# Expert tiles of a mixture layer: weights as the loaded operand of gate and up, in a network kernel on one Trainium2 core

## What is computed

```
scores = einsum('bsd,ed->bse', x, w_gate_router)
topk_scores, topk_idx = top_k(scores, 2)
topk_probs = softmax(topk_scores)
weights = sum(topk_probs[..., None] * one_hot(topk_idx, E), axis=-2)
gate = einsum('bsd,efd->bsef', x, w_gate_proj)
up = einsum('bsd,efd->bsef', x, w_up_proj)
hidden = silu(gate) * up
out = einsum('bsef,edf,bse->bsd', hidden, w_down_proj, weights)
```

## Time and profile before

| | |
|---|---|
| median of 3 runs | 1829.79 us (1825.73 to 1830.11) |
| the profiled execution | 1830.81 us, span 1828.9 us |
| TensorE matmuls busy | 1611.4 us, 88% of the span |
| TensorE loads busy | 1223.2 us, 67% |
| VectorE / ScalarE / GpSimd busy | 1174.7 / 916.3 / 599.9 us |
| mean granted clock of TensorE | 0.891 of full speed |
| tile loop, gate and up of the first tile to the last eviction | 913.3 to 1079.6 us |

### The profile page before, as it was taken

The page is one execution under the profiler, slowest core; times in us unless marked ns, Lnnn a source line. Parts: engine busy times, 40 slices in busy tenths (PEclk is TensorE's granted clock), DMA queues, the critical chain, the costliest instruction groups (busy, mean ns, idle before and its releaser), DMA issues. The chain is left out here.

```text
span 1828.9 us, 77444 instructions
## 1 busy us (share of the span) xinstructions
PE 1611.4 (88%) x32043; PEld 1223.2 (67%) x32043; DVE 1174.7 (64%) x4229; ACT 916.3 (50%) x3325; POOL 599.9 (33%) x1805
## 2 busy tenths in 40 slices
PE   6999999999999999896299965788888888699999
PEld 5988999889999998896266532354545555444444
DVE  5777877777787788777644436566565666474231
ACT  5545555445455555545245445367666667532130
POOL 0333333323333333334345444133223223580000
PEclk9999999999999999555599985789888989699999
DMA  6010010200000001202446444000000000040001
GB/s 239 5 49 30 5 52 5 98 33 5 5 4 5 5 22 56 76 22 73 134 138 238 133 169 137 1 2 0 0 0 0 0 0 1 12 128 18 29 1 47
DMA packets 30635, 90.36 MB, mean 49 GB/s; under 512 B 4848, under 2 KB 6000, under 8 KB 30192
## 3 DMA queue, kind: packets, MB, share of 16 engines
q1 hardware_dynamic: 23920, 64.88, 10.4%
q0 software_dynamic: 6400, 20.98, 3.4%
HBM read 66.90 MB, written 18.87 MB: 47 GB/s over the span
## 5 line engine op out<-in xcount | busy, mean ns | idle before, releaser
L363 PE MATMUL bank<-arena 128*128 128x8 f16 x12288 | 500.9, 170 | 25.2 <-issue 14.0
L366 PE MATMUL bank<-arena 128*128 128x16 f16 x12288 | 495.2, 182 | 2.7 <-issue 2.1
L363 PEld LDWEIGHTS bank<-arena 128*128 128x128 f16 x12288 | 414.4, 97 | 57.9 <-ACT bank L459 32.0
L366 PEld LDWEIGHTS bank<-arena 128*128 128x128 f16 x12288 | 411.9, 97 | 4.1 <-issue 3.2
L635 POOL TENSOR_TENSOR arena<-arena 128x16 f32<-128x16 f32 x512 | 116.8, 228 | 565.9 <-DVE arena L566 551.2
L429 ACT ACTIVATE arena<-arena 128x16 f32<-128x16 f32 x512 | 114.4, 223 | 327.4 <-DVE arena L545 327.3
L545 DVE TENSOR_REDUCE arena<-bank 128x16 f32<-128x48 f32 x512 | 99.5, 194 | 105.2 <-PE bank L366 102.4
L556 DVE TENSOR_TENSOR_SCAN arena<-arena,bank 128x64 f32<-128x64 f32 x512 | 146.7, 287 | 21.0 <-ACT arena L429 6.9
L1898 PE MATMUL bank<-arena 128*128 128x512 f16 x704 | 152.3, 379 | 1.7 <-PEq L1419 1.7
L336 PE MATMUL bank<-arena 128*128 128x256 f16 x1008 | 150.4, 277 | 0.8 <-issue 0.7
L1454 PE MATMUL bank<-arena 128*128 128x512 f16 x576 | 144.4, 406 | 4.5 <-DVE arena L1698 4.5
(11 more groups left out here) (201 smaller groups left out, 2699.9 us busy)
## 6 DMA issues: line engine op xcount, KB each, us to landing
arena<-yrows SPq DMA_DIRECT2D x16, 512.0 KB, 4.1
arena<-in_wgu SPq DMA_DIRECT2D x8, 768.0 KB, 4.7
hrows<-arena SPq DMA_DIRECT2D x16, 256.0 KB, 4.1
arena<-in_xtok SPq DMA_DIRECT2D x16, 256.0 KB, 8.0
out_y<-arena SPq DMA_DIRECT2D x16, 256.0 KB, 2.0
arena<-in_wih SPq DMA_DIRECT2D x4, 768.0 KB, 7.5
arena<-in_whh SPq DMA_DIRECT2D x4, 768.0 KB, 5.3
arena<-in_xT SPq DMA_DIRECT2D x3, 1024.0 KB, 5.9
```

The costliest lines, as they stand in the source:

```text
L363: mm = nc.tensor.matmul(dst[:, j * B:(j + 1) * B, 1], w, h[:, 0], start=home not in opened, stop=False, skip_group_check=True)
L366: mm = nc.tensor.matmul(dst[:, j * B:(j + 1) * B, 1:3], w, h.rearrange("p a c -> p c a"), start=home not in opened, stop=False, skip_group ...
```

## The change

Three things change in the expert tiles, and the number of tiles goes from 40 to 39, the most that 4096 pairs and 8 experts can fill.

1. Gate and up take the weights as the loaded operand and x as the moving one, so that the result has the inner columns on partitions and tokens along the columns. The 384 inner columns of an expert are laid out as three blocks of 128: the first 128 of gate, the first 128 of up, and the remaining 64 of both. Each block needs 12 matmuls of 128 columns. The part pairs go in the order (0,0), (1,0), (0,1) inside each k.
2. The hidden values are then already as down needs them: `turn_hidden`, the copy to `hidT` and their semaphores go. The remaining 64 inner columns are kept as high part on partitions 0 to 63 and as low part on partitions 64 to 127 of one block, and the down weights of these columns are loaded twice, on both halves. Down is five matmuls of 128 partitions: high x high, high x low, low x high of the first 128 columns, and two of the rest block, with the high and the low weights. The elementwise work is done in a block of 128x128 and a block of 64x128 (the sigmoid and the gate product in one operation of 256 columns).
3. TensorE turns x of tile i+2 in iteration i, before down of tile i-1; VectorE copies x of tile i+2 in iteration i; ScalarE evicts tile i-1 in iteration i.

```diff
-TILES = 2 * NTOK // P + E
+FR = F - P
+TILES = (2 * NTOK + E * (P - 1)) // P
...
             if n < NDN:
-                return FH, wdn[:, 2 * n * D:2 * (n + 1) * D]
+                return P, wdn[:, 2 * n * D:2 * (n + 1) * D]
...
-                    for h_, w_ in ((0, 0), (0, 1), (1, 0)):
+                    for cols in range(3):
+                        n = 0
                         for k in range(KT):
-                            mm = nc.tensor.matmul(bank[2 + i % 2][:, 0:2 * F], xt[:, i % 2, h_ * KT + k, :],
-                                                  wgus[w_][:, k, bass.ds(e, 1), :], start=(n == 0), stop=(n == 3 * KT - 1))
-                            n += 1
+                            for h_, w_ in ((0, 0), (1, 0), (0, 1)):
+                                mm = nc.tensor.matmul(bank[2 + i % 2][:, cols * P:(cols + 1) * P],
+                                                      wgus[w_][:, k, bass.ds(e, 1), cols * P:(cols + 1) * P],
+                                                      xt[:, i % 2, h_ * KT + k, :], start=(cols == 0 and n == 0),
+                                                      stop=(n == 3 * KT - 1), skip_group_check=True)
+                                n += 1
...
-                    for h_, w_ in ((0, 0), (0, 1), (1, 0)):
-                        for half in range(2):
-                            mm = nc.tensor.matmul(bank[6 + i % 2][:, :], hidT[0:FH, i % 2, h_, half, :],
-                                                  wdns[0:FH, w_, half, bass.ds(e, 1), :], start=(n == 0), stop=(n == 5))
-                            n += 1
+                    for slot, w_, rest in ((0, 0, 0), (0, 1, 0), (1, 0, 0), (2, 0, 1), (2, 1, 1)):
+                        mm = nc.tensor.matmul(bank[6 + i % 2][:, :], hid[:, i % 2, slot, :],
+                                              wdns[:, w_, rest, bass.ds(e, 1), :], start=(n == 0), stop=(n == 4))
+                        n += 1
...
-                for i in range(TILES + 2):
+                for i in range(TILES + 1):
                     if i < TILES:
                         expert[i] = nc.tensor.value_load(own[0:1, i:i + 1], min_val=0, max_val=E - 1)
                         gate_up(i, expert[i])
                     if i == 0:
                         rest_of_tiles()
-                    if 0 < i < TILES + 1:
-                        turn_hidden(i - 1)
-                    if 0 < i < TILES - 1:
-                        turn_x(i + 1)
-                    if i > 1:
-                        down(i - 2, expert[i - 2])
+                    if i < TILES - 2:
+                        turn_x(i + 2)
+                    if i > 0:
+                        down(i - 1, expert[i - 1])
...
-                    A.activation(sg[:, i % 2, :], bank[2 + i % 2][:, 0:F], ACT.Sigmoid, scale=1 / SWX).then_inc(sig_done, 1)
+                    A.activation(sg[:, i % 2], bank[2 + i % 2][:, 0:4 * P].rearrange("p (c t) -> p c t", t=P)[:, 0:3:2, :],
+                                 ACT.Sigmoid, scale=1 / SWX).then_inc(sig_done, 1)
...
-                    A.activation(hid[:, i % 2, 0, :], hf[:, i % 2, :], ACT.Copy).then_inc(hid_hi, 1)
+                    A.activation(hid[0:FR, i % 2, 2, :], hf[0:FR, i % 2, 1, :], ACT.Copy)
+                    A.activation(hid[:, i % 2, 0, :], hf[:, i % 2, 0, :], ACT.Copy).then_inc(hid_hi, 1)
...
+                    V.scalar_tensor_tensor(hf[0:FR, i % 2, 1, :], bank[2 + i % 2][P - FR:P, 2 * P:3 * P], 1 / SW,
+                                           ga[0:FR, 1, :], ALU.mult, ALU.mult)
+                    V.scalar_tensor_tensor(hf[:, i % 2, 0, :], bank[2 + i % 2][:, P:2 * P], 1 / SW, ga[:, 0, :], ALU.mult,
                                            ALU.mult).then_inc(hf_done, 1)
...
-                    V.tensor_tensor(hid[:, i % 2, 1, :], hf[:, i % 2, :], hid[:, i % 2, 0, :],
+                    V.tensor_tensor(hid[P - FR:P, i % 2, 2, :], hf[0:FR, i % 2, 1, :], hid[0:FR, i % 2, 2, :], ALU.subtract)
+                    V.tensor_tensor(hid[:, i % 2, 1, :], hf[:, i % 2, 0, :], hid[:, i % 2, 0, :],
                                     ALU.subtract).then_inc(hid_lo, 1)
...
-                    if 0 < i < TILES - 1:
-                        take_x(i + 1)
+                    if i < TILES - 2:
+                        take_x(i + 2)
```

More of the change, by code:

```diff
@@ L29 @@
 F = 192
-FH = F // 2
-TILES = 2 * NTOK // P + E
+FR = F - P
+TILES = (2 * NTOK + E * (P - 1)) // P
 NG = NTOK // P
@@ L650, in mixed_net_kernel @@
         m = Mem(arena, mc.at)
-        wdns = m.take([2, 2, E, D], F16, FH)
+        wdns = m.take([2, 2, E, D], F16)
         rowu = m.take([TILES], F32).bitcast(U32)
@@ L703, in mixed_net_kernel @@
         xt = m.take([2, 2 * KT, P], F16)
[L704 to L708, removed]
+        hid = m.take([2, 3, P], F16)
+        hf = m.take([2, 2, P], F32)
         yo = m.take([3, D], F32)
+        ga = m.take([2, P], F32)
+        sg = m.take([2, 2, P], F32)
         assert m.at <= base + 8 * KT * GM * P
@@ L739, in mixed_net_kernel @@
         tx_mm, xt_done, gu_mm, sig_done, ga_done = sem("tx_mm"), sem("xt_done"), sem("gu_mm"), sem("sig_done"), sem("ga_done")
-        hf_done, hid_hi, hid_lo, th_mm, hT_done = sem("hf_done"), sem("hid_hi"), sem("hid_lo"), sem("th_mm"), sem("hT_done")
+        hf_done, hid_hi, hid_lo = sem("hf_done"), sem("hid_hi"), sem("hid_lo")
         yt_mm, y_evac = sem("yt_mm"), sem("y_evac")
@@ L872, in gate_up, with down @@
                         pe.wait_ge(hf_done, i - 1)
-                    n = 0
-                    for h_, w_ in ((0, 0), (0, 1), (1, 0)):
+                    for cols in range(3):
+                        n = 0
                         for k in range(KT):
-                            mm = nc.tensor.matmul(bank[2 + i % 2][:, 0:2 * F], xt[:, i % 2, h_ * KT + k, :],
-                                                  wgus[w_][:, k, bass.ds(e, 1), :], start=(n == 0), stop=(n == 3 * KT - 1))
-                            n += 1
+                            for h_, w_ in ((0, 0), (1, 0), (0, 1)):
[4 more added lines that the diff above has]
+                                n += 1
                     mm.then_inc(gu_mm, 1)
-                def turn_hidden(i):
+                def down(i, e):
                     pe.wait_ge(hid_lo, i + 1)
-                    if i >= 2:
-                        pe.wait_ge(hT_done, i - 1)
-                    for part in range(2):
-                        for half in range(2):
[L887 to L893, removed]
                     if i >= 2:
@@ L971, in high_hidden @@
                     if i >= 2:
-                        act.wait_ge(th_mm, i - 1)
-                    A.activation(hid[:, i % 2, 0, :], hf[:, i % 2, :], ACT.Copy).then_inc(hid_hi, 1)
-                def take_hidden(i):
-                    act.wait_ge(th_mm, i + 1)
-                    if i >= 2:
                         act.wait_ge(yt_mm, i - 1)
-                    A.activation(hidT[0:FH, i % 2].rearrange("p a h t -> p (a h t)"),
-                                 bank[4 + i % 2].bitcast(F16)[0:FH, 0:4 * P], ACT.Copy).then_inc(hT_done, 1)
+                    A.activation(hid[0:FR, i % 2, 2, :], hf[0:FR, i % 2, 1, :], ACT.Copy)
+                    A.activation(hid[:, i % 2, 0, :], hf[:, i % 2, 0, :], ACT.Copy).then_inc(hid_hi, 1)
                 def take_y(i):
@@ L1018, in _ @@
                 A.activation(pr[:, :, :], dif[:, :, :], ACT.Sigmoid, scale=1 / SWX).then_inc(probs, 1)
-                for i in range(TILES + 2):
+                for i in range(TILES + 1):
                     if i < TILES:
                         sigmoid(i)
-                    if 0 < i < TILES + 1:
-                        take_hidden(i - 1)
-                    if i < TILES:
                         high_hidden(i)
-                    if i > 1:
-                        take_y(i - 2)
+                    if i > 0:
+                        take_y(i - 1)
                     if i in SPLIT_IN:
@@ L1173, in hidden @@
                     dve.wait_ge(sig_done, i + 1)
-                    V.scalar_tensor_tensor(ga[:, :], bank[2 + i % 2][:, 0:F], 1 / SWX, sg[:, i % 2, :], ALU.mult,
+                    both_gates = bank[2 + i % 2][:, 0:4 * P].rearrange("p (c t) -> p c t", t=P)[:, 0:3:2, :]
+                    V.scalar_tensor_tensor(ga[:, :, :], both_gates, 1 / SWX, sg[:, i % 2], ALU.mult,
                                            ALU.mult).then_inc(ga_done, 1)
                     dve.wait_ge(ga_done, i + 1)
-                    V.scalar_tensor_tensor(hf[:, i % 2, :], bank[2 + i % 2][:, F:2 * F], 1 / SW, ga[:, :], ALU.mult,
+                    V.scalar_tensor_tensor(hf[0:FR, i % 2, 1, :], bank[2 + i % 2][P - FR:P, 2 * P:3 * P], 1 / SW,
+                                           ga[0:FR, 1, :], ALU.mult, ALU.mult)
+                    V.scalar_tensor_tensor(hf[:, i % 2, 0, :], bank[2 + i % 2][:, P:2 * P], 1 / SW, ga[:, 0, :], ALU.mult,
                                            ALU.mult).then_inc(hf_done, 1)
@@ L2011 @@
```

(6 more changed lines are left out.)

## The result

| | before | after |
|---|---|---|
| median | 1829.95 us (4 runs, 1825.73 to 1830.16) | 1855.48 us (4 runs, 1850.24 to 1858.61) |
| profiled execution, span | 1830.81, 1828.9 us | 1854.02, 1852.2 us |

The changed kernel takes 1.0142 times as long (95% interval 1.0114 to 1.0171), 25.5 us by the medians; the forecast was +22.7 us, 1852.5.

What follows compares the result with a forecast made beforehand. TensorE bounds the kernel now; after the change its sequencer would, at 4.7 us a tile against 4.03. Loop +21.5 and routing +1.2 make +22.7 us, from 1829.79 to 1852.5; own range 1843 to 1861, whole range 1838 to 1869.

Steps and rivals of the forecast that it cites:

- The number of operations: Gate and up: TensorE's sequencer makes 24 register operations a tile instead of 8, 936 over 39 tiles.
- The slot: TensorE's sequencer: each register operation takes 114 to 126 ns, taken as 125, so 16 more add 2.00 us a tile.
- TensorE's own 3.50 us: Expert tile: TensorE's stream without the sequencer, 1.98 gate and up + 0.44 x transposes + five down products of 0.216.
- The loop: Tile loop: 37 periods of 4.7 us against 4.03 now, ending at 1101.1 instead of 1079.55, +21.5 us.
- The end of the loop: Last tile: the chain after gate and up, from leaving TensorE through sigmoid and down to eviction, takes 5.3 us.
- The elementwise work: Expert tiles: VectorE 2.3 us and ScalarE 1.7 us a tile, neither near the period; it matters only in the last tile.
- The routing: Before the loop: larger down-weight loads delay ScalarE's waits for row saves by 0 to 2.0 us, taken as 1.2.
- "Issue" ahead of gate and up: Profile sign: TensorE's loads idle before gate and up by "issue", marking a late sequencer; no size given.
- Rival A: Gate and up: register operations don't grow or cost next to nothing; period 3.50 us, total 1807; chance 0.10.
- Rival C: Tile loop: TensorE's granted clock falls in the starved stream; chance 0.03.
- Rival B: Gate and up: a load-matmul pair with real weights costs more than 55 ns; at 97 ns, 1864 us; chance 0.04.

Runs made afterwards that it cites:

- e1: Changed kernel with gate and up reading weights at an address fixed in the program, so without their register operations; 1816.82 us, 0.9920 of the kernel before.
- e3: Kernel before with only 39 tiles and x turned and copied two tiles ahead; 1821.18 us, 0.9953 of the kernel before.
- e5: Kernel before with 39 tiles, x two tiles ahead and moving gate-up weights in three blocks of 128 columns (24 register operations); 1862.11 us, ratio 1.0157.
- e6: Kernel before with 39 tiles, x two ahead, three hidden-value transposes, five down products, scatter two tiles later in GpSimd's queue; 1814.02 us, ratio 0.9898.

## Why the prediction was right

- **The number of operations.** 936 at the gate-up line, 24 for each of 39 tiles, as counted from 4 k, 2 parts and 3 blocks:

```profile
L877 PEldq FUSED_REGOPS  x936: 46/46/60, 914.4 to 1098.5; - x188
```

- **The slot.** In the tile above 24 operations start within 3.0 us. The forecast of 2.8 + 2.0 - 0.13 = 4.7 met 4.70 in that tile and 4.75 in the mean from tile 1 on. The remainder is operations that start 0.15 us and more after the last instead of 0.125; I had put them in the range, not in the sum. The 24 additional pairs show no price of their own in the slots: an operation with two pairs behind it and one with a single pair both take 0.124 us in the median.
- **TensorE's own 3.50 us.** e1's tile shows 2.01 + 0.45, and the changed kernel 1.10 for down: 3.56. The trace of e1 has 56 ns per pair, over 36 pairs in a row, where the forecast took 55. In the changed kernel the spacing is 87 ns in the mean, but by e1 it is the sequencer's doing.
- **The loop.** +21.5 forecast, +22.9 measured. 37 periods at 4.75 for 4.7 make 1.9 us; the first tile and the end, together 0.5 shorter than forecast, take part of it back.
- **The end of the loop.** The last tile's chain was put at 5.3 us. The last gate-up matmul starts at 1098.6 and the last eviction ends at 1102.92 + 0.69 = 1103.6, so it took 5.0. The order of the steps is that of the prediction:

```profile
1098.84 0.38 ACT L957 ACTIVATE arena<-bank 128x256 f32<-128x256 f32 x1 [2.14 <-PE bank L877]
1099.26 0.42 DVE L1157 SCALAR_TENSOR_TENSOR arena<-bank,arena 128x256 f32<-128x256 f32 x1 [2.50 <-ACT arena L957]
...
1101.63 1.25 PE L893 MATMUL bank<-arena 128*128 x5 [1.56 <-DVE arena L1168]
1102.92 0.69 ACT L973 ACTIVATE arena<-bank,arena 128x512 f32<-128x512 f32 x1 [1.49 <-PE bank L893]
```

- **The elementwise work.** 256 columns take 425 ns on VectorE (0.42 forecast), a half of 128 takes 292 (0.29).
- **The routing was mis-sized:** +1.2 forecast, -0.6 measured. ScalarE's wait for the row saves went from 12.1 to 12.4 us only:

```profile
  DMA hrows<-arena: 12.4, 5
```

The first gather starts 58.8 us after the routing does, where it was 58.7; the 0.6 us lie behind it, as its rows were there for the first transposes after 4.2 us instead of 4.8. In the seven experiments this distance is 4.1 to 4.8 too, and e3 and e5, without the larger pieces, start the first gather after 59.3 and 57.7 us. So what the larger pieces cost is below what differs between executions, and the price of 1.2 us has nothing to show for it. I had multiplied a landing time by a number of waits without asking what each wait ended on.
- **"Issue" ahead of gate and up**, which I had named as a mark of the mechanism, is no mark: the kernel before has it too.
- **Rival A** (no growth) is what e1 shows: tiles of 3.54 us, and 1816.82 us, 10 above the 1807 of the rival, for the most part since some of its tiles wait for hidden values, which I had ruled out only for a period of 4.7. **Rival C** (the clock) didn't happen: the granted clock in the starved loop is 1.00. What a fall would have cost there, against which I had set the upper end of the whole range, no run shows. **Rival B** fell with e1, at 56 ns a pair.

## What to carry to other kernels

Count what the sequencer must do beside the matmuls. In these runs an address from a register costs TensorE's sequencer a slot of about 0.125 us for each different offset, and a wait of its own about 0.10; one or two matmuls of 128 columns at 55 ns can't cover a slot, one of 384 columns at 163 ns can. A cut into shorter matmuls with more addresses can thus lose more than the transposes and products that it saves. When TensorE does get faster, look next at the queue that feeds it: here a gather stood behind a scatter, and only its order had to change.

## What the runs showed that was not expected

- Instructions of the sequencer have irregular gaps. The periods of the changed kernel are spread from 4.6 to 4.9 in most tiles, and their mean from tile 1 on is 0.05 us over that of the tile shown. In e1, with no operations in gate and up, the tiles over 3.54 us wait ahead of down for the low part of the hidden values. Why that part is late stays open: ahead of the tile shown, ScalarE starts the sigmoid after 1.88 us of idle time whose end the profile doesn't explain. e6 suggests GpSimd's queue, but e1 was not run with the later scatter.
- The granted clock stayed at 1.00 in the loop with matmuls 87 ns apart in gate and up, as in e6 with TensorE busy all the time.
